# Who raises the semaphore of a finished bank: the addition itself, or TensorE's sequencer behind a drain

## What is computed

```python
src, dst = edge_index
edge_input = concatenate([x[src], edge_attr])           # 96 + 32 features
messages = gelu(edge_input @ mW1 + mb1) @ mW2 + mb2
gates = sigmoid(gelu(edge_input @ gW1 + gb1) @ gW2 + gb2)
aggregated = segment_sum(messages * gates, dst)
update = gelu(concatenate([x, aggregated]) @ uW1 + ub1) @ uW2 + ub2
h = layernorm(x + update)
```

## Time and profile before

| | |
|---|---|
| median of 3 runs | 5404.54 us (5398.22 to 5406.49) |
| the profiled execution | 5409.02 us, span of its profile 5407.2 us |
| gated message pass | first gather 1524.3 us, last gelu 3794.5 us |
| busy in the whole span | TensorE 78%, VectorE 64%, GpSimd 60%, ScalarE 41% |
| mean granted TensorE clock | 0.88 of 2.4 GHz |

### The profile page before, as it was taken

How to read it: one execution, slowest core, us unless ns; L and a number is a source line. 1 busy time by engine, 2 the same in 40 slices (tenths; PEclk the granted TensorE clock), 3 DMA queues, 4 the chain that set the end, 5 groups by cost and what they waited for, 6 DMA issues and landing times.

```text
span 5407.2 us, 94817 instructions
## 1 busy us (share of the span) xinstructions
PE 4217.6 (78%) x35340; PEld 2569.2 (48%) x35340; DVE 3456.3 (64%) x5455; ACT 2200.9 (41%) x4155; POOL 3239.7 (60%) x2920
## 2 busy tenths in 40 slices
PE   4899899999965566656666565656479999999999
PEld 3888899999943333323333332323333333333333
DVE  6999533544344444444444444444379999999999
ACT  4999200101011111111111111111168888888887
POOL 3699100000046666666666666666358888888888
PEclk9999999999977777787777777777689999999999
DMA  3344899698833334343344344343111221122121
GB/s 71 162 195 195 323 363 370 252 397 336 327 97 113 116 117 120 120 120 113 119 121 120 111 123 119 118 121 111 36 42 57 58 63 57 57 66 57 57 64 38
DMA packets 296568, 760.27 MB, mean 141 GB/s; under 512 B 81160, under 2 KB 183752, under 8 KB 289992
## 3 DMA queue, kind: packets, MB, share of 16 engines
q1 hardware_dynamic: 217496, 595.47, 30.3%
q0 software_dynamic: 78768, 160.85, 11.1%
HBM read 589.77 MB, written 166.38 MB: 140 GB/s over the span
## 4 chain that ended last, share of the span: by engine, by line
PE 55%; another core or an unknown queue 16%; issue 14%; DVE 7%; ACT 4%; POOL 2%; DMA 1%; DVEq 1%; SPq 0%; ACTq 0%; POOLq 0%
PE p_e L1167 15%; PE p_tr L1325 10%; PE p_e L1310 9%; PE p_e L1199 4%; PE p_e L1209 4%; PE p_mm L1287 3%; PE p_tr L1209 2%; ACT GA L1601 2%; PE p_tr L1199 2%; POOL VA L788 1%; PE p_mm L1098 1%; DVE VA L2417 1%; PE p_tr L1026 1%; PE p_mm L1209 1%
## 5 line engine op out<-in xcount | busy, mean ns | idle before, releaser
L788 POOL DMA_INDIRECT GA<-table_mg,VA x1568 | 1493.2, 952 | 1720.0 <-DMA table_mg<-VA 957.8
L2417 DVE TENSOR_TENSOR VA<-VA,p_mm 128x1024 f32<-128x1024 f32 (+1 forms) x1204 | 1362.2, 1208 | 6.1 <-POOL VA L902 5.0
L902 POOL TENSOR_SCALAR VA<-VA 128x1024 f32<-128x1024 f32 (+1 forms) x1204 | 1235.9, 1045 | 168.7 <-ACT VA L1655 155.8
L1199 PE MATMUL p_e<-BD,EA 128*128 128x384 f32 x896 | 467.5, 610 | 492.2 <-ACT GA L1601 266.9
L1655 ACT ACTIVATE VA<-p_e 128x1024 f32<-128x1024 f32 x602 | 616.0, 1023 | 178.1 <-PE p_e L1310 174.5
L1325 PE MATMUL p_tr<-VA,GA 128*32 128x512 f32 (+1 forms) x5096 | 641.3, 580 | 2.7 <-ACT GA L1675 2.1
L1601 ACT ACTIVATE GA<-p_e 128x384 f32<-128x384 f32 x448 | 214.8, 490 | 985.9 <-remote 601.1
L2264 DVE SCALAR_TENSOR_TENSOR R<-R,keep,M 128x97 f32<-128x97 f32 x1568 | 512.6, 327 | 126.1 <-issue 11.7
L2246 DVE TENSOR_TENSOR M<-GA,p_mm 128x1344 f32<-128x1344 f32 x112 | 174.1, 1554 | 653.1 <-issue 348.2
L1199 PEld LDWEIGHTS p_e<-BD,EA 128*128 128x128 f32 x896 | 193.6, 232 | 712.4 <-issue 383.4
L1310 PE MATMUL p_e<-T,GA 32*128 32x512 f16 x4632 | 443.4, 379 | 1.8 <-DVE GA L2386 1.1
(11 more groups left out here) (265 smaller groups left out, 6552.3 us busy)
## 6 DMA issues: line engine op xcount, KB each, us to landing
GA<-adj SPq DMA_DIRECT2D x98, 800.0 KB, 6.1
VA<-adj SPq DMA_DIRECT2D x98, 800.0 KB, 6.2
run_m<-R SPq DMA_DIRECT2D x112, 700.0 KB
GA<-adj SPq DMA_DIRECT2D x98, 768.0 KB, 6.1
VA<-adj SPq DMA_DIRECT2D x98, 768.0 KB, 6.1
H<-adj SPq DMA_DIRECT2D x56, 896.0 KB, 5.1
adj<-GA SPq DMA_DIRECT2D x25, 1568.0 KB, 5.3
adj<-VA SPq DMA_DIRECT2D x24, 1568.0 KB, 5.3
```

Of the source, the lines that this page charges most:

```text
L788: pool.indirect_dma_start(out=to, out_offset=None, in_=of, in_offset=bass.IndirectOffsetOnAxis(ap=at, axis=0)).then_inc(s, 16)
L902: pool.tensor_scalar(e, e, HIGH, LOW, ALU.min, ALU.max).then_inc(clipped, 1)
L1199: mm = pe.matmul(p_h[k][0:CH, 0:4 * D], EA[:, n % 2, k // 2, :], BD[:, 2 * (k % 2):2 * (k % 2) + 2, :, :].rearrange("p a b f -> p (a b f)" ...
L2417: dve.tensor_tensor(e, e, p_mm[n % 2][:, 0:cols_of(n)].unsqueeze(1).to_broadcast([P, 2, cols_of(n)]), ALU.mult).then_inc(weighed, 1)
```

## The change

The addition no longer carries the increment of `hidden_ready`. TensorE executes a drain behind it, and then its sequencer raises the semaphore. Nothing else is different; `edge_product` still rides on the matmul of line 1199.

```diff
                     n, k = m // BANKS, m % BANKS
                     pe.wait_ge(rows_landed[n % 2][k], 32 * (n // 2 + 1))
                     pe.matmul(p_h[k][0:CH, 0:4 * D].rearrange("p (a f) -> p a f", a=2), C[0:CH, C_ID:C_ID + CH],
-                              G[0:CH, n % 2, 2 * k:2 * k + 2, 0:2 * D], start=False, stop=True
-                              ).then_inc(hidden_ready, 1)
+                              G[0:CH, n % 2, 2 * k:2 * k + 2, 0:2 * D], start=False, stop=True)
+                    pe.drain()
+                    pe.sem_inc(hidden_ready, 1)
```

## The result

The changed kernel takes 5419.68 us (median of six runs, 5409.24 to 5421.65), the kernel before beside it 5401.38 (six runs, 5390.36 to 5406.49). The ratio is 1.0033, with an interval of 1.0018 to 1.0047: slower by some 18 us. The forecast was 5129, so the direction was wrong; the measured time lies within the range.

What follows compares the result with a forecast made beforehand. GpSimd was taken as nearest to a bound in the gated message pass, standing 289 us beyond its gathers' pace. 5409.0 - 265 - 11 = 5133, less 4.5 for the median: 5129 us (chance 0.57); 8-in-10 range 5105 to 5560.

Steps and rivals of the forecast that it cites:

- the start-up of 19.8 us: GpSimd's standing before 1579.26, while TensorE is still in the stage before; 19.8 us not counted as gain.
- Step (a): Gated message pass: a sequencer increment isn't held, so every hold on hidden_ready goes; gain 265 us on GpSimd.
- rival 1: The completion is held, not the increment, so the drain waits as long with TensorE idle; 5850 us or more, chance 0.20.
- Step (b): End of the pass: last gelu about 3.5 us behind the last gather's end instead of 14.7; gain 11 us.
- Step (c): TensorE: 784 drains and sequencer increments cost 0.34 us a bank high, 0.45 low, hidden under the gathers' 2.51.
- the third rival: A sequencer's increment is held the same way, the drain prompt: 5400 to 5500 us; within 0.2% chance 0.05, slower 0.03.
- Rival 2: The drain keeps TensorE's clock low, 3.01 us a bank, making TensorE the bound: 5549 us, chance 0.10.
- Rival 4: Part of the holds stays, by edge_product or shortened: half the gain, 5265 us, chance 0.05.
- The sign that would tell: Rival 1's mark in the trace: TensorE stands 5 to 10 us between an addition and the next edges.
- The point from which it should cost: Rival 1 decides once a drain waits longer than the 0.9 us that the gathers' pace leaves a bank.

Runs made afterwards that it cites:

- Experiment 1: Kernel before plus a drain behind each addition, hidden_ready's increment staying on the addition: 5416.36 us against 5397.21, ratio 1.0036.
- experiment 2: Kernel before plus a spare increment by TensorE's sequencer that nobody waits for, without a drain: 5396.90 us against 5397.21, ratio 1.0001.
- experiment 8: Kernel before with both matmuls of a bank reading only the upper bf16 half of each float32: 5377.52 us against 5398.81, ratio 0.9962.
- experiment 18: Kernel before with a GpSimd memset of 128 by 256 values behind every second gather: 5394.05 us against 5396.85, ratio 0.9994.

## Why the prediction came out wrong

**What bounds the pass.** I took GpSimd's 289 us beyond its pace as the gain that becomes free once its waits end sooner. The amount was right, and so was the pace: without holds the gathers take 1968.4 us for the 1965 of rows 2. Without holds the kernel takes 5072, 57 us under the forecast, because the start-up of 19.8 us goes nearly as well, and time in other stages with gathers too: from the last scan of the pass to the first matmul of the attention, a stage with 49 more gathers, it is 158 us instead of 189, and the first gather starts at 1512 to 1525 us in the profiles of the free condition and at 1521 to 1534 in those of the held one.

**Step (a), the one that failed.** "If an increment of TensorE's sequencer isn't held, every hold goes." The sequencer's increment isn't held: the gelus start 0.04 to 0.1 us behind the drain's end in nearly all banks. But the drain in front of it is held, up to 8.2 us beyond the modelled end of its addition. Experiment 1 shows it late where the riding increment is late (188 of 200 banks), and later by up to 2.1 us. Rows 5 and 6 had shown several banks released within 1.1 us, and I read this as increments set free in a bundle. It was as well the picture of completions that are told in a bundle. The trace could not decide, since a matmul's end in it is modelled and not recorded; I gave the forecast 0.57 on a reading of how it looked. Its record of the semaphore has the four rises at 2433.60, 2433.66, 2433.72 and 2433.78. Four banks of 1.29 us or more can't have ended 0.06 us apart, so at least the first of them had been done earlier and were told late. That argument against rival 1 was a good one, as far as it went; what it left out is that a drain waits for the late telling just as well.

**Step (b), the tail,** went the other way. The last gather ends at 3786.8 and the last gelu starts at 3808.2, 21.4 us behind it where rows 3 and 4 have 14.7. In the free condition it is 4.7 us (3481.75 to 3486.45), beside the 3.5 of the estimate.

**Step (c), the drain's own cost,** was sized right. From one addition to the next at the high clock level it is now 2535.27 - 2533.64 = 1.63 us with the drain, the 1.29 + 0.34 of the sum. In the free condition it is hidden, as costed: 5071 against 5075 us. In the held condition it is not quite hidden; experiments 1 and 2 give 19 us for the drain and nothing for the increment. That is 24 ns of the 340 a bank. Single profiles don't place these 19 us. The pass from first to last gather was not longer in the one of the changed kernel.

**Rival 1** had the mechanism and the wrong price, 5850 or more. It added up TensorE's work, the drains and the whole 1041 us of ScalarE's waits, as though the holds stayed the same length when TensorE stops running ahead. They did not: 693 us of holds, in 207 banks, were left between addition and drain. The banks came through at 2.87 us as before, whatever lay between. The missing rival was: the drain is held as long, and the pass stays as it is, since something other than GpSimd's and TensorE's own work sets its pace already (experiments 8 and 18). Its time would have been that of the third rival, 5400 to 5500, where the result lies. The third rival's own claim, a prompt drain with a late increment, is refuted.

**Rival 2** did not come: the clock went up, 0.77 to 0.82, and to 0.93 in the free condition. **Rival 4** had no part.

**The sign that would tell** was named rightly: stands of TensorE of 5 to 10 us between an addition and the next edges. There they are, 5.82 us at 2541.91. The point from which it should cost, a drain 0.9 us late, was wrong: 188 were later than that and the pass did not grow.

The page that spoke against the change was right. The Trainium skill (PSUM — Partial Sum Buffer, section Engine vs sequencer instructions) has the riding increment fire on completion and the drain wait for an idle engine. Experiment 1 agrees that a drain tells nothing sooner: both came late, nearly always at the same banks, with single drains of up to 10.4 us, and where they differed by more than 0.4 us it was the increment that came first.

## What to carry to other kernels

Before putting a signal in another way, put the new instruction beside the old one with nobody waiting for it: one run tells whether both are late together. When an engine seems to be the bound because it is nearly always busy or standing, slow it by a known amount; if the time does not move, it is waiting at someone else's pace, and more buffers or run-ahead for it will not help either. And measure a kernel beside its rival on the same chip, one after the other: here the condition of the chip was worth 330 us, eighteen times the change.

## What the runs showed of the hardware

- While GpSimd works through indirect gathers, TensorE's completions can come late, for riding increments and drains alike. Single drains lasted up to 10.4 us, and ScalarE waited up to 10.7 us for a riding increment. Where TensorE runs ahead, the lateness of several banks adds up: one gelu of the kernel before starts 29.4 us behind the modelled end of its addition, at 1630.28. It happened with float32 and bf16 matmuls, with half the bytes, and with 14 or 21 banks of run-ahead; it was not seen without gathers, nor with plain transfers from the same engine and queue.
- This depends on the condition met. It was there in four groups of experiments (the kernel before at 5397.21, 5398.81, 5392.85 and 5396.85) and absent in three between them (5072.25, 5075.33, 5071.94). The numbers of the chips were 14, 7, 10 and 12 where it was there, and 8, 7 and 9 where it was absent. Number 7 stands in both lists, but whether that was the same piece isn't known.
- What the cause is stays open. Why a gather holds completions, why the rises of semaphores are recorded so sparsely in the same condition, what sets the 2.86 us a bank, and what ends a single hold were not settled: of the 207 held drains of the changed kernel a third ended with GpSimd over 2.5 us behind its last gather's start, but others ended in the midst of gathers. Nor was a gather into anything but on-chip memory tried, or whether profiling has a part in single holds (the times of all runs, profiled or not, fall in the same two groups).
- A drain of TensorE behind each bank made a bank 1.63 us instead of 1.29 at the high clock level. Of this 68 us in all showed in the time of the kernel with hardly any gathers, nothing where gathers bound the pass (5071 for 5075 us), and 19 us where completions were late.
